# Value matmuls of a head pair in four column groups, with the halves of the sum added on the way back

## The chip, the cores and the metric

The kernel runs on one core of one Trainium2 chip. The metric is the device time of one execution in microseconds. Nothing outside the core takes part: the other cores are idle, and there is no communication.

## The reference, cut to what matters

The program computes a block of four stages on x of shape (4, 512, 128), each with a layernorm before it and a residual add behind it: attention, a routed feed-forward layer of eight experts, a scan, and the feed-forward layer again. The change is in the attention:

```python
q, k, v = (x @ W.T, split into 16 heads of 8) for the three weights
q, k = rope(q), rope(k)
scores = einsum('bhqd,bhkd->bhqk', q, k) / 8 + causal mask
attn = softmax(scores, axis=-1)
out = einsum('bhqk,bhkd->bhqd', attn, v)     # 512 keys, 8 columns per head
x = x + out.transpose @ Wo.T + bo
```

The other three stages come after it and are computed by the same instructions in both kernels.

## The kernel before, in words

**Stages.** Attention takes the first third of the span. It goes through 32 head pairs (`PAIRS`, numbered n = 8a + p for batch a and pair p). Then come the feed-forward layer, the scan and the second feed-forward layer.

**One head pair.** The order is written out by hand in each engine's program. TensorE (PE) does, in the loop over n:

1. `scores(n + 1, 0)` and `scores(n + 1, 1)`: the scores of the next pair, queries on the partitions, only to find each row's maximum on VectorE (DVE, `row_max`, then `split_max`, which writes the maxima into `q_tok`).
2. `queries_with_max(n)`: four transposes of the queries with their maxima (L929 in this place, "Q2T" below). They wait for `split_done`. ScalarE (ACT) copies the result (L703).
3. `weigh_values(n - 1)`: the value matmuls of the pair before (L1003, "V" below). They wait for the last exponentials of that pair.
4. `scores_T(n, 0)`, `scores(n + 1, 2)`, `scores_T(n, 1)`: the transposed scores with the maxima subtracted (L978 with the mask matmuls L983; the first unit is "T0" below, the last "T2"). ACT takes their exponentials (L710) into `probs`.
5. for even n from 2 on, `weighed_T(n // 2 - 1)` (L1012): the transposes of the weighted values of two pairs ("W" below), after ACT has copied them out of PSUM (L715). DVE divides them by the sums (L1405, L1406).
6. `scores_T(n, 2)`, and in some pairs the projections, transposes and output matmuls of the next or the last batch.

**What V computes.** For each of the four key tiles j (512, 384, 256 and 128 query columns, since the mask is causal) and both heads h of the pair, one fp32 matmul with the values as the stationary operand (128 keys x 16 columns: 8 values, a column of ones that gives the softmax sum, zeros) and the probabilities as the moving one. An fp32 matmul is two passes on PE, each a weight load (LDWEIGHTS) and a MATMUL; in the built program both passes of head 0 stand before both passes of head 1. Head h of an even pair writes PSUM partitions 32h to 32h + 15, that of an odd pair 64 + 32h on: one column group of the array for each, so that in a pair two of the four groups are in use. Two pairs (a quad) share the bank `PV_BANK`.

**Slots.** Scores, transposed scores and all other attention results on PE go through a ring of three slots of two PSUM banks each (`RING`), in the order of `ring_order`; PE waits for `slot_free` before it writes and for nothing else there.

**Beside it.** For n < 8 DVE also looks for the maxima of the expert weights (`find_tops`), at n = 10 it sets their scales, and for n = 12 to 27 ACT and DVE split these weights into two parts (L746, L1441). At the end of a batch DVE takes the next layernorm. GpSimd (POOL) does the rotary step of the next batch, and at the start clears the padded tensors, `v_tok` among them (L523, L525). SP issues the loads in one queue, and at their end two fills of `rows_dram` with zeros from a row of `grids` (L472), which are needed by the first scatter after the attention.

Of the kernel before, what the change touches and what calls it, by code (L numbers as in the profile page):

```python
# [25 lines left out]
F = 512  # L26
# [8 lines left out]
HP = H // 2  # L35
# [59 lines left out]
NT = 2 * B * L // P + E - 1  # L95
# [16 lines left out]
SPARE_AT = TOK_AT + B * TT  # L112
FILL_AT = SPARE_AT + NT
GRIDS = FILL_AT + ROW

# [62 lines left out]
def hybrid_block_kernel(nc, x_in, wqkv_in, wo_in, bo_in, w1_in, b1_in, w2_in, b2_in, wg_in, gate_rows_in,  # L178
                        a_in, bm_in, cm_in, dv_in, wdt_in, conv_in, win_in, win_rows_in, wout_in, b1e_in, grids_in,
                        counts_in,  # L180
                        cos_in, sin_in, ident_dram, neg_eye_in, mask_qk_in, mask_kq_in, out):
    with ExitStack() as ctx:  # L182
        def sb(name, shape, dt=F32):
            return ctx.enter_context(nc.sbuf_tensor(name, shape, dt))

        def sem(name):
            return ctx.enter_context(nc.semaphore(name))
# [58 lines left out]
        max_rest = sb("max_rest", [P, TT, 2])  # L246
        v_tok = sb("v_tok", [P, 2, TT, H, VW])

# [27 lines left out]
        tiles_to = sb("tiles_to", [P, E])  # L276
        expert_of = sb("expert_of", [P, NT])
        tiles_past = sb("tiles_past", [P, NT])
        first_row = sb("first_row", [P, NT])
# [3 lines left out]
        list_end = sb("list_end", [P, NT])  # L283
        result_row = sb("result_row", [P, YT])
# [18 lines left out]
        def part(t, at, shape, dt=F32):  # L303
# [4 lines left out]
            return (flat if dt == F32 else flat.bitcast(dt)).rearrange(f"p ({names}) -> p {names}", **sizes)  # L308

        probs_words = probs[:].rearrange("p a b c -> p (a b c)")  # L310
        xf = part(heads_arena, 0, [2, TT, D])
# [28 lines left out]
        b1e = rope_s[:].rearrange("p t d -> p (t d)")[0:3 * E, 0:F]  # L340
        v_words = v_tok[:].rearrange("p a t h w -> p (a t h w)")
        qk_words = qk_sb[:].rearrange("p t d -> p (t d)")
# [44 lines left out]
        goes_to_ready = sem("goes_to_ready")  # L387
        scale_rows_ready = sem("scale_rows_ready")
        zeroed = sem("zeroed")
        post_step = sem("post_step")  # L390
# [30 lines left out]

        attn_loads = [(wqkv, wqkv_in), (cos, cos_in), (sin, sin_in), (neg_eye, neg_eye_in), (mask_qk, mask_qk_in),
                      (mask_kq, mask_kq_in), (wo, wo_in), (bo, bo_in)]
# [19 lines left out]
        def slot_of(unit):  # L443
            return TURN[unit] % RING
# [12 lines left out]
        def _(sp):  # L457
# [9 lines left out]
            for dst, src in scan_loads:  # L467
                sp.dma_start(whole(dst), src).then_inc(scan_in, 16)
            sp.wait_ge(ffn_in, 16 * len(ffn_loads))
            fill = grids[:, FILL_AT:FILL_AT + ROW].bitcast(I32)  # L470
            for r in range(FFNS):
                sp.dma_start(rows_dram[r].ap().rearrange("(n p k) d -> p n (k d)", p=P, k=2),  # L472
                             fill.unsqueeze(1).broadcast_to([P, ROWS // (2 * P), ROW])).then_inc(zeroed, 16)
            sp.wait_ge(slot_free[slot_of(("wo", B - 1))], filled(("wo", B - 1)))
# [34 lines left out]
        def _(pool):  # L509
# [4 lines left out]
            nc.gpsimd.memset(minus_half[:], -0.5).then_inc(pads_set, 1)  # L514
            nc.gpsimd.memset(bias_rows[:].bitcast(I32), 0)
            nc.gpsimd.memset(ones[:], 1.0)
# [179 lines left out]
        def _(act):  # L696
# [198 lines left out]
        def _(pe):  # L895
# [92 lines left out]
            def weigh_values(n):  # L988
                a, p = divmod(n, HP)
                if p == 0:  # L990
                    read_by(("v", a))
                if n == 0:
                    pe.wait_ge(pv_cleared, 1)
                if n >= 2 and n % 2 == 0:
                    pe.wait_ge(weighed_ready, n // 2)
                read_by(("T", n, 2))
                for u in range(3):
                    at = PROB_AT[u]
                    for j in PROB_UNITS[u]:
                        size = L - P * j  # L1000
                        for h in range(2):
                            quadrant = OW * (2 * (p % 2) + h)
                            mm = pe.matmul(ps[quadrant:quadrant + VW, PV_BANK, j * P:L], v_tok[:, a % 2, j, 2 * p + h, :],  # L1003
                                           probs[:, n % 2, h, at:at + size], start=(j == 0), stop=(j == TT - 1))
                        at += size
                mm.then_inc(pv_made, 1)

            def weighed_T(g):
                to = give(("w", g))
                pe.wait_ge(weighed_ready, g + 1)  # L1010
                for t in range(TT):
                    mm = pe.transpose(ps[:, to, t * P:(t + 1) * P], weighed[:, t * P:(t + 1) * P], ident[:])  # L1012
                mm.then_inc(slot_full[slot_of(("w", g))], 1)
# [277 lines left out]
        def _(dve):  # L1291
# [107 lines left out]
            def divide(g):  # L1399
                a, q = divmod(g, 4)  # L1400
                of = take(("w", g))
                if q == 0 and a >= 1:
                    dve.wait_ge(slot_full[slot_of(("at", a - 1))], filled(("at", a - 1)))
                sums = ps[:, of, :].rearrange("p (t h w) -> p t h w", t=TT, h=Q)
# [379 lines left out]
def shape_constants():  # L1784
# [6 lines left out]
    def table(a):  # L1791
        a = np.broadcast_to(a.reshape(TT, P, 1, HD), (TT, P, 2, HD)) * scale
        return a.transpose(1, 0, 2, 3).astype(np.float32)

    def halves(a):
# [15 lines left out]
        "grids": grids, "counts": np.stack([later, np.ones((P, P))], 1).astype(mybir.dt.np(BF16)),  # L1811
        "cos": table(cos), "sin": table(sin), "ident": np.eye(P, dtype=np.float32),
        "neg_eye": halves(NEG_ROOT * np.eye(P)),
# [46 lines left out]
```

## Time and profile before

| | us |
|---|---|
| runs shown | 892.85, 895.38, 888.28 (median 892.85) |
| profiled execution, its own time | 894.25 |
| its span | 892.4 |
| outside the span | 1.85 |
| attention | the first 284 us of the span |
| mean granted TensorE clock | 0.81 of full speed |

The busy shares of the page are averages over four unlike stages. For this change only the attention stage counts, so the views below are of windows inside it. A row of a timeline merges neighbouring instructions of one kind: its first number is the start of the first, the second the time until the modelled end of the last, so the distance between two starts is the safer measure.

### The profile page before, as it was taken

To read this page: it belongs to the slowest core of one execution; us is meant where nothing else is said; L and a number is where in the kernel's file an instruction comes from. 1 tells how busy PE (TensorE), PEld (TensorE's weight loads), DVE (VectorE), ACT (ScalarE), POOL (GpSimd) and SP (SyncE) were. 2 spreads that over 40 slices of the span, in tenths; PEclk is the share of its full clock that TensorE was granted. 3 is DMA by queue.
4 is the path that set the end of the run, shared out by engine and by line. 5 is a ranking of instruction groups with operands and counts; after the bars stand their busy time and mean duration, and the time that the engine had idled before them with its cause. 6 is when DMAs were issued, how large, how long until landed. Compare 5 with 4: busy or idle time off the path is not lost. (4 is left out here: it accounts for less than half of the span.)

```text
span 892.4 us, 16950 instructions
## 1 busy us (share of the span) xinstructions
PE 594.1 (67%) x5836; PEld 402.2 (45%) x5836; DVE 466.1 (52%) x1241; ACT 344.4 (39%) x462; POOL 349.9 (39%) x447
## 2 busy tenths in 40 slices
PE   2588888888885635578776750567676588676730
PEld 1454445444443413466655640234354376555520
DVE  5877776776772555533222221678867543222214
ACT  1355456556652424335332320225254354332310
POOL 4152080190001575534544453114335445444550
PEclk9699999999997757789877785667687799877875
DMA  8995000000000000111110102100000111111104
GB/s 297 328 334 161 2 1 1 1 2 1 1 2 27 24 7 28 38 45 38 31 31 25 37 19 77 35 0 25 7 19 24 35 46 32 31 30 31 35 18 150
DMA packets 45146, 46.37 MB, mean 52 GB/s; under 512 B 5369, under 2 KB 42386, under 8 KB 44810
## 3 DMA queue, kind: packets, MB, share of 16 engines
q1 hardware_dynamic: 40522, 35.91, 13.5%
q0 software_dynamic: 4544, 9.38, 3.1%
q8 instruction: 52, 0.85, 0.4%
q14 instruction: 28, 0.23, 0.1%
HBM read 16.75 MB, written 28.52 MB: 51 GB/s over the span
## 5 line engine op out<-in xcount | busy, mean ns | idle before, releaser
L1650 DVE COPY arena<-ps 128x128 f32<-128x128 f32 x78 | 22.7, 292 | 211.3 <-DMA y_dram<-arena,goes_to 177.4
L831 ACT ACTIVATE arena<-ps,up_back 128x512 f32<-128x512 f32 x78 | 53.6, 687 | 194.5 <-PE ps L1194 194.5
L1194 PE MATMUL ps<-arena,w 128*128 128x128 f16 x936 | 96.6, 246 | 45.3 <-DVE arena L1636 45.0
L1384 DVE TENSOR_REDUCE row_maxima<-ps 128x2 f32<-128x256 f32 (+3 forms) x128 | 99.0, 817 | 42.8 <-PE ps L958 42.5
L710 ACT ACTIVATE probs<-ps 128x768 f32<-128x768 f32 (+1 forms) x96 | 82.5, 884 | 81.2 <-PE ps L983 81.2
L512 POOL TENSOR_TENSOR rstd<-var_eps,minus_half 128x4 f32<-128x4 f32 x16 | 17.0, 1060 | 222.6 <-DVE var_eps L1321 222.6
L1205 PE MATMUL ps<-w,probs 128*128 x936 | 95.2, 248 | 10.8 <-DVE probs L1642 10.7
L1194 PEld LDWEIGHTS ps<-arena,w 128*128 x936 | 72.2, 106 | 65.9 <-issue 55.5
L661 POOL DMA_INDIRECT y_dram<-arena,goes_to x78 | 85.0, 1090 | 34.5 <-POOL goes_to L654 20.9
L643 POOL DMA_INDIRECT rows_dram<-probs,idx x64 | 69.0, 1078 | 52.8 <-DVE idx L1582 33.0
L1205 PEld LDWEIGHTS ps<-w,probs 128*128 128x128 f16 x936 | 77.0, 111 | 21.9 <-issue 12.3
L652 POOL TENSOR_SCALAR result_row<-qk_sb,list_end 128x1 f32<-128x1 f32 x78 | 29.4, 377 | 132.0 <-DMA y_dram<-arena,goes_to 120.9
L1003 PE MATMUL ps<-probs,v_tok 128*16 128x256 f32 (+3 forms) x512 | 74.7, 434 | 2.5 <-ACT probs L710 2.5
L1642 DVE SCALAR_TENSOR_TENSOR probs<-arena,hid_scale,probs 128x512 f16<-128x512 f32 x78 | 58.2, 746 | 4.5 <-ACT probs L836 4.5
L836 ACT ACTIVATE probs<-arena,hid_scale 128x512 f16<-128x512 f32 x78 | 56.3, 721 | 2.6
L1189 PE MATMUL ps<-which,bias_rows 128*128 128x128 bf16 x312 | 37.4, 254 | 20.4 <-issue 20.0
L654 POOL TENSOR_SCALAR goes_to<-result_row,grids 128x1 int32<-128x1 f32 x78 | 46.7, 599 | 7.3
L1003 PEld LDWEIGHTS ps<-probs,v_tok 128*16 128x16 f32 x512 | 24.2, 96 | 47.7 <-issue 35.4
L953 PE MATMUL ps<-heads_arena 48*128 48x128 bf16 (+3 forms) x256 | 37.6, 308 | 11.6 <-DVE row_maxima L1384 6.4
L978 PE MATMUL ps<-q2T,heads_arena 50*128 50x512 bf16 (+3 forms) x256 | 38.5, 310 | 9.0 <-ACT probs L710 7.2
L1189 PEld LDWEIGHTS ps<-which,bias_rows 128*128 128x128 bf16 x312 | 22.1, 112 | 32.2 <-issue 31.4
L1159 PE MATMUL ps<-w,arena 128*128 128x128 f16 x384 | 26.2, 230 | 13.3 <-DVE arena L1616 8.9
(234 smaller groups left out, 1111.7 us busy)
## 6 DMA issues: line engine op xcount, KB each, us to landing
rows_dram<-grids SPq DMA_DIRECT2D x2, 8840.0 KB, 44.1
qk_sb<-rows_dram SPq DMA_DIRECT2D x78, 65.0 KB, 1.8
arena<-in_w SPq DMA_DIRECT2D x2, 2304.0 KB
arena<-y_dram SPq DMA_DIRECT2D x8, 512.0 KB, 4.0
y_dram<-arena,goes_to POOLq DMA_INDIRECT x78, 2.4
x_all<-in_x SPq DMA_DIRECT2D x4, 256.0 KB, 8.1
rows_dram<-probs,idx POOLq DMA_INDIRECT x64
out_x<-x_all SPq DMA_DIRECT2D x4, 256.0 KB, 3.7
```

Of the source, the lines that this page charges most:

```text
L643: nc.gpsimd.indirect_dma_start(rows_dram[r].ap(), bass.IndirectOffsetOnAxis(ap=idx[:, r, b, t, k:k + 1], axis=0), xrow_words[:, b % 2, t, ...
L654: nc.gpsimd.tensor_scalar(goes_to[:, n % YT:n % YT + 1], result_row[:, n % YT:n % YT + 1], grids[:, SPARE_AT + s:SPARE_AT + s + 1], None, ...
L661: nc.gpsimd.indirect_dma_start(y_dram.ap(), bass.IndirectOffsetOnAxis(ap=goes_to[:, n % YT:n % YT + 1], axis=0), y_t[:, n % YT, :], None). ...
L710: nc.scalar.activation(probs[:, n % 2, :, PROB_AT[u]:PROB_AT[u] + size], ps[:, of:of + 2, 0:size], ACT.Exp).then_inc(slot_free[slot_of(("T ...
L831: nc.scalar.activation(hid_t[:, n % HT, :], ps[:, of, :], ACT.Gelu, scale=up_back[:]).then_inc(bank_free[of], 1)
L836: nc.scalar.activation(hid16_t[:, n % HT, 0, :], hid_t[:, n % HT, :], ACT.Identity, scale=hid_scale[:]).then_inc(high_t_ready, 1)
L1003: mm = pe.matmul(ps[quadrant:quadrant + VW, PV_BANK, j * P:L], v_tok[:, a % 2, j, 2 * p + h, :], probs[:, n % 2, h, at:at + size], start=( ...
L1189: pe.matmul(ps[:, to, c * P:(c + 1) * P], bias_rows[:, c * P:(c + 1) * P], which[:, s:s + 1].broadcast_to([P, P]), start=(c == 0), stop=Fa ...
L1194: mm = pe.matmul(ps[:, to, c * P:(c + 1) * P], w1[:, w, bass.ds(expert[s], 1), c * P:(c + 1) * P].rearrange("p o f -> p (o f)"), xgT[:, (r ...
L1205: mm = pe.matmul(ps[:, to, 0:D], hid16_t[:, n % HT, v, c * P:(c + 1) * P], w2[:, w, bass.ds(expert[s], 1), c, :].rearrange("p o d -> p (o ...
L1384: ins = nc.vector.tensor_reduce(row_maxima[:, t, 2 * p:2 * p + 2], ps[:, of:of + 2, o:o + keys], AX.X, ALU.max)
L1642: nc.vector.scalar_tensor_tensor(hid16_t[:, n % HT, 1, :], hid_t[:, n % HT, :], hid_scale[:], hid16_t[:, n % HT, 0, :], ALU.mult, ALU.subt ...
```

## The change

- The values are laid out with 41 words for each key tile and head of two neighbouring pairs: values and a one at 0 to 8 for the even pair, at 32 to 40 for the odd pair, zeros between. The stationary operand is now 32 columns wide. For an even pair it starts at 0, for an odd pair at 16, so that the odd pair's values stand in columns 16 to 24 and zeros in 0 to 15.
- The column group of a matmul is given by head and half of the key tiles: tiles 0 and 3 in one half, 1 and 2 in the other. Both pairs of a quad accumulate into the same four groups.
- Each head's sum then stands in two halves. The way back is no longer a transpose but a matmul with the constant `fold` of ones and zeros (128 x 64), which adds the halves while it turns them. It is an ordinary fp32 matmul, two passes for each of the four query tiles, and writes 64 columns for each tile, not 128.
- ACT copies the values of a batch in two instructions, not one. POOL clears 2640 words of `v_tok`, not 2048, and sets the ones in two instructions.
- `fold` is one more load among the first constants. The zeros for `rows_dram` now come from `bias_rows`, cleared at the start, so that the fills no longer wait for the loads of the feed-forward layer; `grids` is 260 words a row shorter. Four small tables of the tile map share the memory of `weighed`, which is free by then.

```diff
+VS = 2 * VW + HD + 1
+
+HALVES = ((0, 3), (1, 2))
...
-        v_tok = sb("v_tok", [P, 2, TT, H, VW])
+
+        v_flat = sb("v_tok", [P, 2 * TT * HP * VS + VW])
+        v_tok = v_flat[:, 0:2 * TT * HP * VS].rearrange("p (a t g w) -> p a t g w", a=2, t=TT, g=HP)
+        fold = sb("fold", [P, Q * VW])
...
-            sp.wait_ge(ffn_in, 16 * len(ffn_loads))
-            fill = grids[:, FILL_AT:FILL_AT + ROW].bitcast(I32)
+            sp.wait_ge(zero_set, 1)
+            words = ROWS * ROW // (2 * P)
+            size = max(n for n in range(1, F // 2 + 1) if words % n == 0)
+            fill = bias_rows[:, 0:2 * size].bitcast(I32)
...
-            nc.gpsimd.memset(v_tok[:], 0.0).then_inc(pads_set, 1)
+            nc.gpsimd.memset(v_flat[:], 0.0).then_inc(pads_set, 1)
             pool.wait_ge(pads_set, 4)
-            nc.gpsimd.memset(v_tok[:, :, :, :, HD:HD + 1], 1.0).then_inc(pads_set, 1)
+            nc.gpsimd.memset(v_tok[:, :, :, :, HD:HD + 1], 1.0)
+            nc.gpsimd.memset(v_tok[:, :, :, :, 2 * VW + HD:2 * VW + HD + 1], 1.0).then_inc(pads_set, 1)
...
-                nc.scalar.copy(v_tok[:, a % 2, :, :, 0:HD],
-                               ps[:, of, :].rearrange("p (t h d) -> p t h d", t=TT, h=H)).then_inc(slot_free[slot_of(("v", a))], 1)
+                for q in range(2):
+                    ins = nc.scalar.copy(v_tok[:, a % 2, :, :, 2 * VW * q:2 * VW * q + HD].rearrange("p t (g h) d -> p (t g) h d", h=2),
+                                         ps[:, of, :].rearrange("p (g q h d) -> p q g h d", q=2, h=2, d=HD)[:, q])
+                ins.then_inc(slot_free[slot_of(("v", a))], 1)
...
-                for u in range(3):
-                    at = PROB_AT[u]
-                    for j in PROB_UNITS[u]:
-                        size = L - P * j
-                        for h in range(2):
-                            quadrant = OW * (2 * (p % 2) + h)
-                            mm = pe.matmul(ps[quadrant:quadrant + VW, PV_BANK, j * P:L], v_tok[:, a % 2, j, 2 * p + h, :],
-                                           probs[:, n % 2, h, at:at + size], start=(j == 0), stop=(j == TT - 1))
-                        at += size
+                at = {j: PROB_AT[u] + sum(L - P * i for i in PROB_UNITS[u] if i < j) for u in range(3) for j in PROB_UNITS[u]}
+                for j in range(TT):
+                    half = 0 if j in HALVES[0] else 1
+                    for h in range(2):
+                        group = OW * (2 * half + h)
+                        at_v = (((a % 2) * TT + j) * HP + p // 2 * 2 + h) * VS + VW * (p % 2)
+                        mm = pe.matmul(ps[group:group + OW, PV_BANK, j * P:L],
+                                       v_flat[:, at_v:at_v + OW],
+                                       probs[:, n % 2, h, at[j]:at[j] + L - P * j],
+                                       start=(p % 2 == 0 and j == HALVES[half][0]), stop=(j == HALVES[half][1]), skip_group_check=True)
                 mm.then_inc(pv_made, 1)
...
-                    mm = pe.transpose(ps[:, to, t * P:(t + 1) * P], weighed[:, t * P:(t + 1) * P], ident[:])
+                    mm = pe.matmul(ps[:, to, t * Q * VW:(t + 1) * Q * VW], weighed[:, t * P:(t + 1) * P], fold[:], start=True, stop=True)
```

The order of the instructions on PE stays. This is V of a pair in the program before, with what stands around it (the sizes are those of the result, partitions x columns; in brackets the semaphores waited for):

```order
L929 MATMUL ps<-ident,q_tok 128x128 [waits split_done]
L929 MATMUL ps<-ident,q_tok 128x128 x3
L1003 MATMUL ps<-probs,v_tok 16x512 [waits slot_free1]
L1003 MATMUL ps<-probs,v_tok 16x512
L1003 MATMUL ps<-probs,v_tok 16x384 x2
L1003 MATMUL ps<-probs,v_tok 16x256 x2
L1003 MATMUL ps<-probs,v_tok 16x128 x2
L978 MATMUL ps<-q2T,heads_arena 128x512 [waits q2T_ready,slot_free0]
```

And the same place in the changed program, where V is L1012:

```order
L938 MATMUL ps<-ident,q_tok 128x128 [waits split_done]
L938 MATMUL ps<-ident,q_tok 128x128 x3
L1012 MATMUL ps<-probs,v_tok 32x512 [waits slot_free1]
L1012 MATMUL ps<-probs,v_tok 32x512
L1012 MATMUL ps<-probs,v_tok 32x384 x2
L1012 MATMUL ps<-probs,v_tok 32x256 x2
L1012 MATMUL ps<-probs,v_tok 32x128 x2
L987 MATMUL ps<-q2T,heads_arena 128x512 [waits q2T_ready,slot_free0]
```

The tiles come in the same order, two heads each; what differs is that the pairs of 384 and 256 columns now go to the two column groups that the pairs of 512 and 128 leave free.

## Rows read from the trace of the kernel before

**Rows 1.** The page: the span, and the granted TensorE clock in 40 slices.

```profile
span 892.4 us, 16950 instructions
...
PEclk9699999999997757789877785667687799877875
```

**Rows 2.** Stretches: length, busy time by engine (instructions), clock, DMA.

```profile
172.50:281.00 108.50, 90.33 (x1130) 50.65 (x1126) 68.81 (x130) 63.25 (x85) 20.10 (x27) 1.00 0.01 1
281.00:893.00 612.00, 379.27 (x3220) 275.90 (x3220) 271.27 (x842) 201.47 (x279) 272.90 (x340) 0.74 0.12 34
```

**Rows 3.** Timeline of PE, pairs 28 and 29: start, length, instructions [idle before].

```profile
253.64 0.39 PE L978 MATMUL ps<-q2T,heads_arena 50*128 50x512 bf16 x2
...
255.83 0.63 PE L1012 MATMUL ps<-ident,weighed 128*128 128x128 f32 x4 [1.08 <-ACT weighed L715]
256.39 0.28 PE L978 MATMUL ps<-q2T,heads_arena 50*128 50x256 bf16 x2
...
257.96 2.33 PE L1003 MATMUL ps<-probs,v_tok 128*16 128x512 f32 x16
260.22 0.39 PE L978 MATMUL ps<-q2T,heads_arena 50*128 50x512 bf16 x2
...
263.16 0.40 PE L929 MATMUL ps<-ident,q_tok 128*128 128x128 bf16 x4
263.49 2.33 PE L1003 MATMUL ps<-probs,v_tok 128*16 128x512 f32 x16
```

**Rows 4.** Timeline of PE's weight loads inside one V.

```profile
202.47 0.12 PEld L1003 LDWEIGHTS ps<-probs,v_tok 128*16 128x16 f32 x4
202.91 0.10 PEld L1003 LDWEIGHTS ps<-probs,v_tok 128*16 128x16 f32 x2 [0.33 <-issue]
203.34 0.10 PEld L1003 LDWEIGHTS ps<-probs,v_tok 128*16 128x16 f32 x2 [0.33 <-issue]
203.66 0.10 PEld L1003 LDWEIGHTS ps<-probs,v_tok 128*16 128x16 f32 x2 [0.22 <-issue]
```

**Rows 5.** The same V's instructions in a stretch of its first 0.04 us.

```profile
202.46:202.50 0.04, 0.03 (x2) 0.03 (x4) 1.00 0.00 0
```

**Rows 6.** Timeline of PE: eight fp32 passes with 8 and with 128 moving columns.

```profile
302.72 1.06 PE L1120 MATMUL ps<-wg,heads_arena 128*128 128x8 f32 x8
303.64 0.38 PE L1148 MATMUL ps<-ident,route 128*9 128x128 f32 x2
...
243.64 1.16 PE L1026 MATMUL ps<-wo,attT 128*128 128x128 f32 x8
244.73 0.23 PE L953 MATMUL ps<-heads_arena 48*128 48x128 bf16 x2
```

**Rows 7.** Timelines of DVE and ACT beside rows 3.

```profile
261.10 1.22 DVE L1384 TENSOR_REDUCE row_maxima<-ps 128x2 f32<-128x1024 f32 x1 [1.82 <-PE ps L958]
...
262.88 0.18 DVE L1397 CAST q_tok<-max_rest 128x8 bf16<-128x8 f32 x1
...
260.77 2.50 ACT L710 ACTIVATE probs<-ps 128x1024 f32<-128x1024 f32 x3 [2.18 <-PE ps L983]
263.60 0.59 ACT L703 COPY q2T<-ps 128x512 bf16<-128x512 bf16 x1 [0.33 <-PE ps L929]
```

**Rows 8.** Timeline of PE: pairs in which DVE ends the wait behind V.

```profile
102.39 0.39 PE L953 MATMUL ps<-heads_arena 48*128 48x512 bf16 x2 [2.02 <-DVE row_maxima L1384]
...
128.26 0.39 PE L953 MATMUL ps<-heads_arena 48*128 48x512 bf16 x2 [1.17 <-DVE row_maxima L1384]
...
194.82 0.40 PE L929 MATMUL ps<-ident,q_tok 128*128 128x128 bf16 x4 [0.71 <-DVE q_tok L1397]
```

**Rows 9.** Timelines of POOL and PE at the start.

```profile
12.03 1.90 POOL L523 MEMSET v_tok<- 128x2048 f32 x1
...
14.07 0.48 PE L908 MATMUL ps<-ident,xn 128*128 128x128 f32 x1 [1.18 <-DVE xn L1327]
```

**Rows 10.** The instructions of ACT's copy of the values: duration min/median/max.

```profile
L728 ACT COPY v_tok<-ps x4: 586/591/592, 19.7 to 180.1; 128x512 f32<-128x512 f32 x4
```

More of the change, by code:

```diff
@@ L112 @@
 SPARE_AT = TOK_AT + B * TT
-FILL_AT = SPARE_AT + NT
-GRIDS = FILL_AT + ROW
+GRIDS = SPARE_AT + NT
 BANKS = 8
@@ L180, in hybrid_block_kernel @@
                         counts_in,
-                        cos_in, sin_in, ident_dram, neg_eye_in, mask_qk_in, mask_kq_in, out):
+                        cos_in, sin_in, fold_in, ident_dram, neg_eye_in, mask_qk_in, mask_kq_in, out):
     with ExitStack() as ctx:
@@ L308, in part @@
             return (flat if dt == F32 else flat.bitcast(dt)).rearrange(f"p ({names}) -> p {names}", **sizes)
+        expert_of, tiles_past, first_row, list_end = (weighed[:, NT * i:NT * (i + 1)] for i in range(4))
         probs_words = probs[:].rearrange("p a b c -> p (a b c)")
@@ L340, in hybrid_block_kernel @@
         b1e = rope_s[:].rearrange("p t d -> p (t d)")[0:3 * E, 0:F]
-        v_words = v_tok[:].rearrange("p a t h w -> p (a t h w)")
+        v_words = v_flat[:]
         qk_words = qk_sb[:].rearrange("p t d -> p (t d)")
@@ L388, in hybrid_block_kernel @@
         scale_rows_ready = sem("scale_rows_ready")
+        zero_set = sem("zero_set")
         zeroed = sem("zeroed")
@@ L420, in hybrid_block_kernel @@
         out_dram = out.rearrange("b (t p) d -> b p t d", p=P)
-        attn_loads = [(wqkv, wqkv_in), (cos, cos_in), (sin, sin_in), (neg_eye, neg_eye_in), (mask_qk, mask_qk_in),
+        attn_loads = [(wqkv, wqkv_in), (cos, cos_in), (sin, sin_in), (fold, fold_in), (neg_eye, neg_eye_in), (mask_qk, mask_qk_in),
                       (mask_kq, mask_kq_in), (wo, wo_in), (bo, bo_in)]
@@ L468, in _ @@
                 sp.dma_start(whole(dst), src).then_inc(scan_in, 16)
-            sp.wait_ge(ffn_in, 16 * len(ffn_loads))
-            fill = grids[:, FILL_AT:FILL_AT + ROW].bitcast(I32)
+            sp.wait_ge(zero_set, 1)
+            words = ROWS * ROW // (2 * P)
+            size = max(n for n in range(1, F // 2 + 1) if words % n == 0)
+            fill = bias_rows[:, 0:2 * size].bitcast(I32)
             for r in range(FFNS):
-                sp.dma_start(rows_dram[r].ap().rearrange("(n p k) d -> p n (k d)", p=P, k=2),
-                             fill.unsqueeze(1).broadcast_to([P, ROWS // (2 * P), ROW])).then_inc(zeroed, 16)
+                sp.dma_start(rows_dram[r].ap().rearrange("(p k) d -> p (k d)", p=P).rearrange("p (n w) -> p n w", w=size),
+                             fill.unsqueeze(1).broadcast_to([P, words // size, size])).then_inc(zeroed, 16)
             sp.wait_ge(slot_free[slot_of(("wo", B - 1))], filled(("wo", B - 1)))
@@ L514, in _ @@
             nc.gpsimd.memset(minus_half[:], -0.5).then_inc(pads_set, 1)
-            nc.gpsimd.memset(bias_rows[:].bitcast(I32), 0)
+            nc.gpsimd.memset(bias_rows[:].bitcast(I32), 0).then_inc(zero_set, 1)
             nc.gpsimd.memset(ones[:], 1.0)
@@ L1403, in divide @@
                     dve.wait_ge(slot_full[slot_of(("at", a - 1))], filled(("at", a - 1)))
-                sums = ps[:, of, :].rearrange("p (t h w) -> p t h w", t=TT, h=Q)
+                sums = ps[:, of, 0:TT * Q * VW].rearrange("p (t h w) -> p t h w", t=TT, h=Q)
                 core_link(nc.vector.reciprocal(rec[:], sums[:, :, :, HD]))
@@ L1811, in shape_constants @@
         "grids": grids, "counts": np.stack([later, np.ones((P, P))], 1).astype(mybir.dt.np(BF16)),
-        "cos": table(cos), "sin": table(sin), "ident": np.eye(P, dtype=np.float32),
+        "cos": table(cos), "sin": table(sin),
+        "fold": np.tile(np.eye(Q * VW, dtype=np.float32).reshape(2, 2, VW, Q * VW).transpose(1, 0, 2, 3).reshape(Q * VW, Q * VW), (2, 1)),
+        "ident": np.eye(P, dtype=np.float32),
         "neg_eye": halves(NEG_ROOT * np.eye(P)),
```

4 lines of the change are left out of this document (removed).

## The prediction

> **What bounds the kernel now.** I began with the page: the span, the clock and the shares [rows 1]. The shares mix four stages, so the next view was busy time by stretch. In 108.5 us of attention PE is busy for 90.3, DVE for 68.8, ACT for 63.3, at full clock; behind 281 the clock is granted at 0.74 on average [rows 2]. Nothing in that second part is changed, so it should only move forward. The question is whether attention ends earlier.
>
> The timeline of PE answers what a pair costs [rows 3]. From the T0 of pair 28 to that of pair 29 it is 260.22 - 253.64 = 6.58 us (even pairs, with W), and from V to V one pair on 263.49 - 257.96 = 5.53 (odd pairs). V holds PE from 257.96 to the next T0 at 260.22, thus 2.26 us of each, and T0 stands right behind it. The views of DVE and ACT beside it [rows 7] show the loop: T0 at 260.22, exponentials from 260.77 to 263.27, maxima split at 262.88 + 0.18 = 263.06, Q2T at 263.16, V at 263.49. All of this hangs on T0; V alone hangs on nothing but its place, and T0 on V. So a shorter V shortens the loop one for one, until something that does not hang on T0 is late.
>
> **V itself.** Its weight loads show the steps [rows 4]: four at 202.47, two at 202.91, 203.34 and 203.66, each pair with the start of a pass in both heads. A pass takes 0.43 us for 512 columns (both steps) and 0.32 for 384; so 0.215 and 0.11 for 256 and 128 by the same rate. Before, a group has all eight passes: 2 x (0.43 + 0.32 + 0.215 + 0.11) = 2.15, and 0.11 until T0 starts. After, heads' groups of tiles 0 and 3 have 2 x (0.43 + 0.11) = 1.08, those of tiles 1 and 2 have 2 x (0.32 + 0.215) = 1.07. If all four groups run at once V takes **1.08 + 0.11 = 1.2 us, 1.07 less**. The trace never has more than two groups at work, so bounds: 1.2 from below (each group must do its passes); 2.26 from above, since no more is asked than that heads keep running side by side as now. The weight loads are 32 columns for 16; they lie under the passes.
>
> Whether the groups run at once depends on order. In the program both passes of head 0 come before head 1, yet two passes start within the first 0.04 us and four weight loads with them [rows 5]: head 1's first pass went past head 0's second, which waited for its own group. With four groups it has to go past two and three waiting passes. The Trainium skill, "TensorE: Matmul & The Clock Gate", Part 3, The mechanism, says instead that matmuls are "pc-monotone in start AND end", in strict order. By that rule the steps would be a chain in which only neighbours overlap, and V would stay near what it is. The start of two passes of different heads in 0.04 us speaks against it, so I take 1.2. A middle case is that only two passes may wait in front: then tiles 1 and 2 start at 0.43, and V ends after 0.43 + 2 x 0.32 + 2 x 0.215 + 0.11 = 1.6 us.
>
> V is on the path in 32 pairs: 32 x 1.07 = **34.2 us** at most.
>
> **W.** The transposes hold PE from 255.83 to 256.39, 0.56 us for four single passes [rows 3]. The new ones are eight fp32 passes with a 128-column stationary operand and 64 moving columns. Eight with 8 moving columns take 303.64 - 302.72 = 0.92, eight with 128 take 244.73 - 243.64 = 1.09 [rows 6]: the weight load, not the moving side, sets the step of about 0.11. I take 1.0 (the bounds are these two rows), 0.44 more. W stands on the path: T2 waits behind it, the last exponential behind T2, V behind that. 16 x 0.44 = **7.0 us back** (5.8 to 8.5). The same page's table of terms calls transpose mode "4× faster for FP32". By that, W would take 4 x 0.56 = 2.24 and the price be 27 us; rows 6 have an ordinary fp32 tile at twice a transpose, not four times, because the load bounds both.
>
> In the quad's other chain, DVE divides 0.44 later. In pair 28 its results are due when the third slot of the scores is given out, about the time it gets there now; I put up to 0.05 on it, nothing in the sum.
>
> **Where the 1.07 does not arrive.** With V shorter, work that does not shrink comes to the front.
> - At two batch ends DVE is the path behind V: S waits 2.02 us for it at 102.39, from a chain of layernorm and weight maxima begun before V [rows 8]; a like wait stands at the second end. At 128.26 it waits 1.17 for the scales set at n = 10. V's gain there is lost whole: 3 x 1.07 = 3.2.
> - Elsewhere DVE sits idle before its last maximum. Where that is over 1.07 (1.82 at 261.10 [rows 7]) nothing is lost, and ACT has room too: its query copy ends at 263.60 + 0.59 = 264.19, V now would end at 264.7. In pairs with weight splits or maxima on DVE the idle time is shorter; the worst case is at 194.82, where Q2T already waits 0.71 for DVE [rows 8]. Going pair by pair I lose about 0.8 there, 0.5 before the first batch end, 0.3 and 0.1 in two others, and 1 us for backlogs in n = 3 to 7 and 19: 2.8 in all.
>
> Sum of losses: **6 us** (4 to 9).
>
> **The small edits.** The larger `v_tok` costs at the start: the clearing takes 1.90 us for 2048 words, and only behind it does DVE give the last piece of the first layernorm to PE at 14.07 [rows 9]. 2640 words take 2.45: **+0.55**, on the path (nothing else is ready). The two settings of ones lie behind that piece. ACT's copy of the values, 0.59 us four times [rows 10], becomes two of half the size, each with its fixed part: between +0 and +0.59 each, I take 0.2 for three batches in pairs that are not bound by ACT, so **+0.3**. `fold` is one more small load in a queue whose constants are in before PE gets to them. The zero fills start where their queue gets to them instead of behind the loads, which are nearly done by then; they are needed hundreds of us later. Nothing for either.
>
> **Sum.** -34.2 + 7.0 + 6 + 0.8 = -20.4. The profiled execution has 894.25, so 873.9 for it; it lies 1.4 above the median of the runs shown, so against the median **873 us** (0.978).
>
> **Rivals.**
> - *Two passes may wait, not three* (V 1.6, 0.66 less): 32 x 0.66 = 21.1, of which DVE takes 2.6, so -21.1 + 2.6 + 7.0 + 0.8 = -10.7: 882. For it: the trace shows one pass passed, no more. 14%.
> - *No overlap beyond now, slower*: V stays at 2.26 and the new groups only change places. Then W and the start are left, +7.0 + 0.8: **901**. It decides from a V above 2.0 (32 x 0.24 = 7.8). For it is the page's rule of strict order; against it rows 5. 8%.
> - *Transposes cheap by four*: W at 2.24, 16 x 1.68 = 27 in place of 7: 893. Against it rows 6. 3%.
> - *The clock*: with less to do PE might fall to the lower of its two levels inside attention, as it does at the batch ends, where it had waited 2.02 for DVE [rows 1, 8]. A pair has about 4 us of PE work then, at half clock 8, so eight such pairs cost 8 x 3.5 = 28, all of the gain: about 901. Against it: even pairs with 1.08 us of waiting keep full clock now. 4%.
> - *DVE takes more*, 12 us instead of 6, because its chains slip together: 879. 8%.
>
> My forecast, four groups at once with these losses, has the remaining 63%, its own range 868 to 878 (W 5.8 to 8.5, losses 4 to 9, runs that spread by 7 us). To hold 8 in 10, the range reaches over the DVE case and most of the middle one: **868 to 884**. What a measurement here can tell from no change is about 1%, thus 883.9 and 901.8. Faster by more: all of the forecast and the DVE case, two thirds of the middle one: 0.79. Within 1%: the rest of the middle one, half of the slower ones, the transposes: 0.13. Slower: 0.08.
>
> **What the profile after would show.** V to T0 in 1.2 us (middle case 1.6), four first passes and up to eight weight loads in its first 0.05 us. W as x8 in 1.0. Odd pairs at 4.5 in place of 5.53, even ones at 5.95 in place of 6.58. The same waits at the ends of the batches, a little longer, since PE comes earlier. Attention ends near 264, not 284, and what follows takes as long as now. I am wrong if V keeps its length, if the clock falls inside a batch, or if waits for DVE or ACT stand before most T1 or V.

## The result and the profile after

The changed kernel takes **883.7 us** (median of 19 runs, 877.3 to 890.6), the kernel before, measured beside it, 891.7: ratio **0.990 [0.988, 0.993]** (the brackets hold a 95% interval). It is faster, but by 8 us and not by the 20 of the forecast. The profiled execution has 887.59 against 894.25, spans 885.8 and 892.4.

The page first, as in [rows 1]:

```profile
span 885.8 us, 17084 instructions
...
PEclk9699899888996767699777775758677799777765
```

A slice is 22 us. In slices 3 to 12, which are attention, stand four 8s where [rows 1] has ten 9s: the granted clock falls inside attention. To keep the start apart from it I read attention from the V of pair 0, V(0), to that of pair 31, V(31). Busy time by stretch, columns as in [rows 2], of before and then of the change:

```profile
45.91:275.37 229.46, 191.93 (x2409) 110.18 (x2407) 160.99 (x320) 131.96 (x172) 63.85 (x86) 0.99 0.16 48
```

```profile
47.53:268.25 220.72, 181.16 (x2468) 120.75 (x2467) 162.37 (x320) 132.44 (x175) 63.92 (x86) 0.91 0.34 61
```

Attention is 8.7 us shorter, at a granted clock of 0.91, not 0.99. V(0) comes 1.6 us later, and from V(31) to the end of the span it is 617.0 us before and 0.5 more now. So -8.7 + 1.6 + 0.5 = -6.6, the span's difference. Nearly all that is missing is missing inside attention.

Is it V? PE's timeline of pairs 28 and 29, as in [rows 3]:

```profile
256.63 1.28 PE L1012 MATMUL ps<-probs,v_tok 128*32 128x512 f32 x16
257.85 0.39 PE L987 MATMUL ps<-q2T,heads_arena 50*128 50x512 bf16 x2
...
260.04 1.08 PE L1022 MATMUL ps<-fold,weighed 128*128 128x64 f32 x8 [1.08 <-ACT weighed L722]
261.05 0.28 PE L987 MATMUL ps<-q2T,heads_arena 50*128 50x256 bf16 x2
```

V to T0 is 257.85 - 256.63 = 1.22 (2.26 in [rows 3]), and W to T2 1.01 (0.56). The weight loads of another V, to be read against [rows 4]:

```profile
97.13 0.16 PEld L1012 LDWEIGHTS ps<-probs,v_tok 128*32 128x32 f32 x8
97.49 0.64 PEld L1012 LDWEIGHTS ps<-probs,v_tok 128*32 128x32 f32 x8 [0.21 <-issue]
```

Eight loads at once where there were four. And V's instructions alone, in its first 0.05 us, against [rows 5]:

```profile
97.12:97.17 0.05, 0.04 (x4) 0.04 (x6) 1.00 0.54 106
```

Four passes where there were two: all four groups are at work. So V and W are as forecast.

Now the place where the clock falls, PE's timeline at the first end of a batch, against [rows 8]:

```profile
98.57 0.28 PE L992 MATMUL ps<-mask_kq,neg_eye 64*128 64x128 bf16 x4
101.93 0.39 PE L962 MATMUL ps<-heads_arena 48*128 48x512 bf16 x2 [3.08 <-DVE row_maxima L1394]
...
103.44 1.97 PE L1022 MATMUL ps<-fold,weighed 128*128 128x64 f32 x8
105.33 0.40 PE L987 MATMUL ps<-q2T,heads_arena 50*128 50x256 bf16 x2
```

PE gets to the wait 1 us sooner, so it waits 3.08 us where it waited 2.02; a little later, at half the clock, the same eight instructions of W take 1.89 us, not 1.01. Four stretches in the view by windows: the wait, what follows it, and two later ones.

```profile
98.35:101.93 3.58, 0.50 (x11) 0.21 (x8) 3.55 (x11) 1.50 (x2) 1.02 (x1) 1.00 1.15 206
105.33:109.00 3.67, 3.67 (x39) 2.63 (x38) 1.34 (x4) 1.40 (x2) 0.38 (x1) 0.50 1.15 195
163.70:167.10 3.40, 3.03 (x20) 2.13 (x20) 2.91 (x6) 0.81 (x1) 0.68 (x1) 0.50 0.02 5
191.00:204.70 13.70, 12.51 (x106) 7.30 (x102) 8.80 (x17) 5.86 (x9) 7.26 (x10) 0.50 0.01 2
```

PE is busy for 0.50 us of the 3.58 in which it waits, and after the fall all the time at 0.50, which is the lower of its two levels, 1.2 GHz. Six such stretches add up to 37.5 us in attention; before there were two, 6.8 us. The longest, 191.0 to 204.7, follows no long wait but short ones (0.97 us until 188.47, 0.36 until 189.33, 0.28 until 190.47).

### The profile page after: what moved, and what is told of

Same layout as the page of the kernel before. It is cut to its first block and busy times, and to the rows that moved or that the text cites. A ratio compares the mean times of both kernels' runs of the same rounds, so it can differ in the third digit from the quotient of the medians.

```text
span 885.8 us, 17084 instructions
## 1 busy us (share of the span) xinstructions
PE 585.2 (66%) x5900; PEld 415.3 (47%) x5900; DVE 467.5 (53%) x1241; ACT 345.0 (39%) x466; POOL 349.8 (39%) x448
## 5 line engine op out<-in xcount | busy, mean ns | idle before, releaser
L1394 DVE TENSOR_REDUCE row_maxima<-ps 128x2 f32<-128x256 f32 (+3 forms) x128 | 98.5, 817 | 26.2 <-PE ps L967 25.6
L1215 PE MATMUL ps<-w,probs 128*128 x936 | 96.0, 250 | 10.8 <-DVE probs L1652 10.4
L518 POOL TENSOR_TENSOR rstd<-var_eps,minus_half 128x4 f32<-128x4 f32 x16 | 17.0, 1061 | 209.8 <-DVE var_eps L1331 209.8
L668 POOL DMA_INDIRECT y_dram<-arena,goes_to x78 | 83.7, 1073 | 32.6 <-POOL goes_to L661 20.9
L659 POOL TENSOR_SCALAR result_row<-qk_sb,weighed 128x1 f32<-128x1 f32 x78 | 30.3, 388 | 141.6 <-DMA y_dram<-arena,goes_to 129.0
L962 PE MATMUL ps<-heads_arena 48*128 48x128 bf16 (+3 forms) x256 | 39.8, 324 | 17.3 <-DVE row_maxima L1394 11.6
L1012 PE MATMUL ps<-probs,v_tok 128*32 128x256 f32 (+3 forms) x512 | 45.4, 476 | 2.3 <-ACT probs L717 2.3
L987 PE MATMUL ps<-q2T,heads_arena 50*128 50x512 bf16 (+3 forms) x256 | 40.7, 326 | 8.4 <-ACT probs L717 4.5
L967 PE MATMUL ps<-mask_qk,neg_eye 64*128 64x128 bf16 x512 | 36.8, 229 | 0.0
L992 PE MATMUL ps<-mask_kq,neg_eye 64*128 64x128 bf16 x512 | 34.8, 230 | 0.0
```

The source lines that it names most:

```text
L659: link(nc.gpsimd.tensor_scalar(result_row[:, n % YT:n % YT + 1], xg_words[:, n % XG, D:D + 1], list_end[:, s:s + 1], xg_words[:, n % XG, D ...
L668: nc.gpsimd.indirect_dma_start(y_dram.ap(), bass.IndirectOffsetOnAxis(ap=goes_to[:, n % YT:n % YT + 1], axis=0), y_t[:, n % YT, :], None). ...
L1215: mm = pe.matmul(ps[:, to, 0:D], hid16_t[:, n % HT, v, c * P:(c + 1) * P], w2[:, w, bass.ds(expert[s], 1), c, :].rearrange("p o d -> p (o ...
L1394: ins = nc.vector.tensor_reduce(row_maxima[:, t, 2 * p:2 * p + 2], ps[:, of:of + 2, o:o + keys], AX.X, ALU.max)
```

## Why does DVE keep PE waiting?

DVE's timeline in pair 2 (L1394 the row maxima, L1404 to L1407 their split for the queries), and under it POOL's in the same stretch, where it rotates the next batch's q and k:

```profile
61.40 3.01 DVE L1394 TENSOR_REDUCE row_maxima<-ps 128x2 f32<-128x256 f32 x4
64.54 1.01 DVE L1404 CAST q_tok<-row_maxima 128x8 bf16<-128x8 f32 x1
65.58 1.06 DVE L1405 TENSOR_TENSOR max_rest<-row_maxima,q_tok 128x8 f32<-128x8 f32 x1
66.68 0.19 DVE L1407 CAST q_tok<-max_rest 128x8 bf16<-128x8 f32 x1
```

```profile
64.35 1.16 POOL L584 TENSOR_TENSOR rope_s<-rope_c,q_tok 128x512 f32<-128x512 f32 x1
65.46 1.15 POOL L585 TENSOR_TENSOR rope_s<-rope_c,k_tok 128x512 f32<-128x512 f32 x1
66.68 0.65 POOL L586 CAST q_tok<-rope_s 128x512 bf16<-128x512 f32 x1
```

Two instructions on eight columns take 1.01 and 1.06 us, and each ends when POOL's does: 64.54 + 1.01 = 65.55 beside 64.35 + 1.16 = 65.51, then 66.64 beside 66.61. The third begins together with POOL's next, at 66.68, and takes 0.19. The four row maxima take 3.01 us beside POOL, and as much where POOL is idle (experiment 7). That is what the Trainium skill, "SBUF — State Buffer", Who interferes with whom, says: the port pair that DVE shares with GpSimd goes to whoever issues first, for the whole instruction, and the other side is fully blocked; among DVE's instructions casts can ask for it, those with two operands in SBUF meet GpSimd's reads there, and reductions don't contend. The trace agrees. Before, the same split took 0.28, 0.62 and 0.54, behind a longer V. Whether this matters is a question for runs.

So the theory is: V and W are right; shorter pairs bring PE to waits that DVE sets, the waits grow, and the clock's falls take about half of what is missing. The rival is that V's gain is worth less than its length (PE shares something when four groups run), or that the fold or the fills cost more than their instructions.

## The experiments

Each ratio is to the kernel before as it was measured beside that kernel: 894.5 us for experiments 1 to 3 and the changed kernel of 4, 893.3 for the control of 4, the first two kernels of 7 and experiment 8, 900.8 for the others. "Attention" is V(0) to V(31) of the profiled execution, and a "half-rate stretch" is one in it at a granted clock of 0.50. Every edit but the control's and the first of 7 is made to the changed kernel.

**1. Two groups, with the fold.** The group goes by head alone.

```diff
-                    half = 0 if j in HALVES[0] else 1
+                    half = 0
...
-                                       start=(p % 2 == 0 and j == HALVES[half][0]), stop=(j == HALVES[half][1]), skip_group_check=True)
+                                       start=(p % 2 == 0 and j == 0), stop=(j == TT - 1), skip_group_check=True)
```

> The changed kernel with one part undone: the column group of a value matmul is given by the head alone, so V has two groups again; fold, layout, start and fills stay as changed. If W and the start were sized right (7.0 and 0.8 us), this is 8 us above the kernel before (ratio 1.009), V takes 2.26 us up to T0 again and W 1.0; the clock then stays full inside a batch as before. If W costs less than thought because its 0.44 us lie beside the waits for DVE, the ratio is 1.003 or below. If the clock falls here too (theory of the clock wrong: it does not come from the shorter V), PE shows half rate in more than the two stretches at the batch ends.

907.3 us, **1.017 [1.013, 1.021]**; even pairs take 7.04, not 6.58 (+0.46). Without four groups the fold is a loss, and larger than expected: 15 x 0.45 = 6.8 us are its length, and the clock costs more here too (attention 237.92 at 0.97 on average, 233.25 with the clock held in experiment 5, so 4.7). The value of four groups is the distance to the change, 1.017 - 0.990.

The expectation had the clock as before. It falls at the same two places, the ends of the batches, and behind the same wait (2.01 us at the first, 2.02 before), but each stretch is twice as long, 13.7 us in all and not 6.8. This is the first:

```profile
104.00:110.70 6.70, 6.34 (x54) 4.70 (x52) 3.45 (x9) 2.21 (x3) 0.38 (x1) 0.50 1.15 198
```

So a part of what the clock costs comes with the other edits (the fold, the start, the copies) and not with the shorter V.

**2. Four groups, no fold.** W is a transpose again.

```diff
-                    mm = pe.matmul(ps[:, to, t * Q * VW:(t + 1) * Q * VW], weighed[:, t * P:(t + 1) * P], fold[:], start=True, stop=True)
+                    mm = pe.transpose(ps[:, to, t * P:(t + 1) * P], weighed[:, t * P:(t + 1) * P], ident[:])
...
-                sums = ps[:, of, 0:TT * Q * VW].rearrange("p (t h w) -> p t h w", t=TT, h=Q)
+                sums = ps[:, of, :].rearrange("p (t h w) -> p t h w", t=TT, h=2 * Q)[:, :, 0:Q, :]
```

> The changed kernel with the four transposes in place of the fold matmuls: the adding of the two halves is left out, half of the sums is divided. W goes back from 1.0 to 0.56 us. Plain pairs: even ones at 5.5 us in place of 5.98. If W is on the path everywhere, 7 us less than the changed kernel (ratio 0.982). If the longer waits of PE for DVE now lower the clock more often, less of it arrives: ratio 0.985 to 0.990, with more time at half rate inside attention than the 38 us of the changed kernel.

877.1 us, **0.983 [0.980, 0.985]**. Even pairs 5.53 in place of 5.98: 0.45 x 16 = 7.2, and 0.0077 x 892 = 6.9 by the ratios, give or take 3. Attention falls by more, from 220.7 to 209.9, since less of it is at half rate: 17 us in four stretches, not 37.5 in six. So what shows W's term is the length of W and of the plain pairs, and the total is only in line with it. The clock falls in more places than before without the fold as well, so the fold is not what starts that; but it lengthens it.

**3. The old shape of the fills.** The zeros come from a wide cleared tile again, at the early place in the queue.

```diff
-            fill = bias_rows[:, 0:2 * size].bitcast(I32)
+            fill = zero_rows[:].bitcast(I32)
...
+                sp.dma_start(rows_dram[r].ap().rearrange("(n p k) d -> p n (k d)", p=P, k=2),
+                             fill.unsqueeze(1).broadcast_to([P, ROWS // (2 * P), ROW])).then_inc(zeroed, 16)
```

> The changed kernel with the zero fills in their old shape (1040 bytes a piece instead of 884, in rows interleaved over the partitions, from a zero row widened by 16 bytes), started where the changed kernel starts them. The fills then end near 86 us again, not near 110. If the longer fills disturb nothing, the ratio is that of the changed kernel, 0.990 within 0.003. If they slow the start or the weights' way, 1 to 3 us less, and V of the first pair starts near 46 us in place of 47.5.

886.2 us, **0.991 [0.989, 0.994]**: the same as the change. Attention took 220.73 in its profile and 220.72 in the change's. The new shape costs nothing, and the two numbers also say how exactly attention repeated here. The earlier place was not undone; in the traces the fills start at 21.4 in the change and at 22.0 before.

**4. The clock held.** Idle matmuls (results never read), 109 in all, where PE waits for DVE by about as long anyway: in loops 4, 5, 8, 11, 16, 19, 20. A control does it to the kernel before, in loops 4, 8, 11, 16.

```diff
+            def keep_busy(n, count):
+                for _ in range(count):
+                    pe.matmul(ps[:, Q2_BANK, (n + 1) % 2 * (L // 2):((n + 1) % 2 + 1) * (L // 2)], ident16[:],
+                              kT[:, n // HP % 2, 0, 0:L // 2], start=True, stop=True)
...
                 scores_T(n, 0)
+                keep_busy(n, {8: 26, 16: 26, 11: 22, 19: 6}.get(n, 0))
...
+                    keep_busy(n, {5: 12}.get(n, 0))
                     scores(n + 1, 1)
+                keep_busy(n, {4: 12, 20: 5}.get(n, 0))
```

> The changed kernel with idle matmuls of 256 bf16 columns (0.107 us each, results overwritten) put where PE waited longest for DVE: 26 in pairs 8 and 16, 22 in pair 11, 6 in pair 19 before the scores of the next pair, 12 and 5 before the query transposes of pairs 4 and 20, 12 in pair 5. Theory of the clock: the changed kernel loses about 10 us to 38 us at half rate inside attention (before 7 us), because PE waits longer; kept busy, the clock stays full, attention ends 8 to 10 us earlier, ratio 0.979 to 0.982. Rival, DVE and GpSimd: the time is lost because DVE is the path in those pairs whatever PE's clock; then the ratio stays at 0.990 or gets worse by what the idle matmuls delay, even with the clock at 1.0.

> Control: the kernel before with idle matmuls in its own longest waits for DVE (17 in pairs 8 and 16, 10 in pair 11, 6 before the query transposes of pair 4). It loses only 7 us to half rate inside attention, so the theory of the clock gives it 1 to 3 us (ratio 0.996 to 1.000), far less than the 11 us that idle matmuls gave the changed kernel. If it gains as much as that one (0.987), the gain there is no matter of what the change did to the clock.

The changed kernel: 874.7 us, **0.978 [0.974, 0.981]**. The control: 889.7 us, 0.996 [0.993, 0.999]. More work for PE makes the changed kernel 1.3% faster. PE's timeline at the same end of a batch, the idle matmuls in place of the wait of 3.08:

```profile
96.03 0.39 PE L987 MATMUL ps<-q2T,heads_arena 50*128 50x512 bf16 x2
96.26 0.28 PE L992 MATMUL ps<-mask_kq,neg_eye 64*128 64x128 bf16 x4
96.47 3.01 PE L1041 MATMUL ps<-heads_arena,ident 128*128 128x256 bf16 x26
99.62 0.39 PE L962 MATMUL ps<-heads_arena 48*128 48x512 bf16 x2
```

and its attention as a stretch:

```profile
46.69:257.37 210.68, 180.11 (x2578) 122.42 (x2576) 164.48 (x320) 132.20 (x175) 63.88 (x86) 0.99 0.37 64
```

From T0 to the next S it is 3.59 us here and 3.58 in the change: DVE sets that time, PE idle or not. But pair 7 as a whole falls from 12.01 to 9.27, pair 15 from 11.88 to 9.43, and attention from 220.7 to 210.7: **10.0 us** of the change are half rate. Before, the control's attention is 228.8 against 229.5, 0.7.

Neither hold is complete. Here one stretch is left, 251.3 to 254.7, and the last step, V(30) to V(31), takes 5.57 us, where it takes 4.25 at full clock in experiments 2 and 9: 1.3 more. In the control the two ends of a batch gain 2.4 (10.26 to 9.11 and 10.47 to 9.26), but a stretch that was not there before begins at 131.8, and one V in it takes 3.74 us and not 2.27. Put right by these, the clock costs the change 11.3 us and the kernel before 2.2: still 9 between them.

**5. Two groups with the clock held** prices V by itself: experiment 1 with 50 idle matmuls.

```diff
-                    half = 0 if j in HALVES[0] else 1
+                    half = 0
...
+                keep_busy(n, {4: 6}.get(n, 0))
...
+                keep_busy(n, {8: 17, 16: 17, 11: 10}.get(n, 0))
```

> Column groups by head only (two at once, as before the change) with the fold kept, and idle matmuls at PE's long waits, so that the clock is held: against 'warm' only the value matmuls differ in the clock-free comparison. If four groups save the 1.07 us of each V to T0 step on the plain path, it is 27 to 33 us above 'warm', ratio 1.008 to 1.015. If with the clock held the gain of four groups were as small as the 8.7 us of the change as a whole plus the fold's 7, it would be 16 us above 'warm', ratio 0.996.

909.6 us, 1.011 [1.006, 1.016]. Its clock stays up through all of attention:

```profile
47.06:280.31 233.25, 201.69 (x2519) 125.09 (x2517) 160.02 (x320) 131.74 (x175) 63.90 (x86) 1.00 0.33 58
```

and V is as long as ever (84.07 to the T0 at 86.35, 2.28):

```profile
84.07 2.35 PE L1012 MATMUL ps<-probs,v_tok 128*32 128x512 f32 x16
86.35 0.39 PE L987 MATMUL ps<-q2T,heads_arena 50*128 50x512 bf16 x2
```

233.3 - 210.7 = 22.6 us, or 23.9 without the stretch that experiment 4 has left, is what four groups give at full clock. The 31 steps are worth 31 x (2.28 - 1.22) = 32.9, so 9 to 10 stand in waits that do not shrink. By ratio it is (1.011 - 0.978) x 892 = 30 us, give or take 5, as expected, but against two measurements of the kernel before, 900.8 and 894.5; why it lies above the traces I can't say, and I take the traces, in which plain pairs agree to 0.02 us. Against the control, 228.8 less 1.5 for its stretch, the fold costs 6.0 us at full clock, near its 6.8. Either way four groups gain more than they seem to in the change as a whole, and the rival of a V that is worth less falls.

**6. Halves with unequal columns.** It asks what sets V's length: tiles 0 and 1 in one half, 2 and 3 in the other.

```diff
-HALVES = ((0, 3), (1, 2))
+HALVES = ((0, 1), (2, 3))
```

> Key tiles 0 and 1 in one half, 2 and 3 in the other, in place of 0 and 3, 1 and 2: the columns of one half are then 512+384 against 256+128 instead of 640 each. If the four groups run side by side and the longest sets the time, V takes 896/640 of what it does: T0 starts 1.6 us after V instead of 1.22, over 31 pairs 9 to 12 us, 893 to 896 us in all, ratio 1.000 to 1.004. If V's time goes by the sum of the columns (the engine takes them one behind another), nothing changes: ratio 0.990.

898.4 us, 0.998 [0.995, 1.000], just under the 1.000 to 1.004 expected. V to T0 is 85.67 - 84.04 = 1.63:

```profile
84.04 1.70 PE L1012 MATMUL ps<-probs,v_tok 128*32 128x512 f32 x16
85.67 0.39 PE L987 MATMUL ps<-q2T,heads_arena 50*128 50x512 bf16 x2
```

The longest group sets V, by its own passes: 2 x (0.43 + 0.32) + 0.11 = 1.61 from the prices of [rows 4]. Plain pairs took 0.41 more, thus up to 12.7 us; by the ratios it is 6.7 us in all, and in attention 4.2, at a clock of 0.95, not 0.91 (21 us at half rate, not 37.5). The length of a step and what it moves in the clock work against each other here.

```profile
48.38:273.29 224.91, 186.03 (x2468) 115.50 (x2467) 162.19 (x320) 132.20 (x175) 63.91 (x86) 0.95 0.33 59
```

**7. Without the rotation on POOL.** The rotary step of batches 1 to 3 is left out, which leaves POOL idle beside DVE.

```diff
-                for t in range(TT):
-                    qk = qk_sb[:, t, :].rearrange("p (k h d) -> p k h d", k=2, h=H)
...
-                nc.gpsimd.tensor_tensor(k_slot(4), kr, k_slot(1), ALU.subtract).then_inc(roped, 1)
+                nc.gpsimd.memset(k_tok[:, 0, 0, 0:1], 0.0).then_inc(roped, 1)
```

> The kernel before without the rotary step of batches 1 to 3 on GpSimd (left out; these batches work on old queries and keys). Theory: small DVE instructions wait while GpSimd works, but in the kernel before most of that is hidden behind V: 1 to 4 us less, ratio 0.995 to 0.999.

> The changed kernel without the rotary step of batches 1 to 3 on GpSimd (left out). Theory of DVE and GpSimd: pairs 3, 4, 11 and 19, where DVE is the path, lose 5 us to DVE instructions that wait for GpSimd, and the drops of the clock behind them another 5; without it the ratio to the kernel before is 0.978 to 0.982 (10 us below the changed kernel), against 1 to 4 us for the same edit in the kernel before. If only the clock at the batch ends matters, 1 to 3 us as there.

> The changed kernel without the rotation of batches 1 to 3 on GpSimd (their q and k are those of batch 0), and idle matmuls only in loops 8 and 16, where PE waits for VectorE by 3 us. It leaves VectorE alone on its port where the rotation stood beside it. Without either, the changed kernel lost 15 us with the rotation taken out and 9 us with the clock held. If the rotation costs mostly by making PE wait until the gate falls, the two overlap: 868 to 871 us, ratio 0.974 to 0.977. If VectorE's slow small instructions cost by themselves, they add up: 860 to 865 us, ratio 0.965 to 0.970.

Before: 887.2 us, 0.993 [0.991, 0.996]. The change: 871.2 us, 0.974 [0.969, 0.978]. The change with idle matmuls in loops 8 and 16: 865.3 us, **0.960 [0.956, 0.965]**. So by the ratios the rotation costs the kernel before 6 us and the changed one 15 (0.9902 - 0.9737); in the traces attention itself loses 3.7 before (229.5 to 225.7). All three ratios lie below the figures that were expected, and the last says that clock and rotation are in the main separate losses: 0.0126 and 0.0165 one by one, 0.0299 together. With the clock held the rotation makes attention 210.7 - 199.9 = 10.8 us longer. The split of pair 2 without it, and attention:

```profile
63.53 0.19 DVE L1376 CAST q_tok<-row_maxima 128x8 bf16<-128x8 f32 x1
63.75 0.17 DVE L1377 TENSOR_TENSOR max_rest<-row_maxima,q_tok 128x8 f32<-128x8 f32 x1
63.96 0.19 DVE L1379 CAST q_tok<-max_rest 128x8 bf16<-128x8 f32 x1
...
46.75:246.66 199.91, 173.10 (x2521) 117.73 (x2519) 150.81 (x320) 131.74 (x175) 5.75 (x8) 0.99 0.38 68
```

0.17 to 0.19 where it was up to 1.06. Pair 2 takes 4.53, with the rotation 6.32, clock held in both; pairs 3, 10, 18 and 19 are shorter by 1.6, 3.4, 1.9 and 1.1. DVE's busy time in attention falls from 164.5 to 150.8. These kernels leave POOL's rotation out as a whole; a rotation that only leaves the port alone was not tried, so that the port is the cause rests on the ends that coincide above.

**8. The start.** POOL clears q_tok, k_tok and v_tok only when the four normalized tiles are there.

```diff
+            pool.wait_ge(xna_ready, TT)
             nc.gpsimd.memset(q_tok[:].bitcast(I32), 0)
```

> The changed kernel, but GpSimd clears q_tok, k_tok and v_tok only once DVE has made the first layernorm (a wait in front of the three). In the changed kernel these clearings hold DVE's four instructions until 14.5 us, 2.4 of it by the larger v_tok. Expected: xn ready at 8 us, PE starts 6 us earlier; the rotary step on DVE then waits for the clearings, which end 1 to 2 us later than now. Net 2 to 4 us less than the changed kernel, ratio 0.986. If all is hidden behind the first loads, no change.

881.9 us, **0.985 [0.980, 0.991]**, an interval that overlaps the change's, and V(0) at 42.3, not 47.5. (The 2.4 us in the expectation are the whole clearing of `v_tok`; its growth is 0.5.) DVE's timeline, in the change and then in this run:

```profile
6.58 7.90 DVE L1337 TENSOR_SCALAR xn<-x_all,mean,rstd 128x128 f32<-128x128 f32 x4 [0.96 <-POOL rstd L518]
```

```profile
6.70 1.12 DVE L1338 TENSOR_SCALAR xn<-x_all,mean,rstd 128x128 f32<-128x128 f32 x4 [0.96 <-POOL rstd L518]
13.49 0.42 DVE L1354 TENSOR_TENSOR rope_c<-ps,cos 128x256 f32<-128x256 f32 x1 [5.68 <-POOL k_tok L529]
```

Four normalizations take 1.12 us alone and 7.90 beside POOL's clears. V(0) comes 5.3 us earlier and the span is 8.6 us shorter than the change's; by the ratios it is 4.3, give or take 5, so that a gain in time is likely but not shown. Four half-rate stretches, 23.9 us, remain.

**9. All that the runs point to.** Idle matmuls as in 4 (with 8 more in loop 30 and 12 ahead of the last V) and the later clears.

> The version that the runs so far point to: the changed kernel, with the idle matmuls of the run 'warm' (plus 8 ahead of the fold of loop 30 and 12 ahead of the last value matmuls, where PE stood longest before the gate fell late in attention), and GpSimd clearing q_tok, k_tok and v_tok only after the four normalized token tiles are there. If the gate and the start are separate losses, they add up: 'warm' took 9 us off the changed kernel and the later clears alone 1.7 to 4 us (V(0) 5 us earlier, part of it lost to more half-rate clock), so 869 us, ratio to before 0.972 to 0.976, V(0) at 42.3 us. If the earlier start only makes the attention wait at the next transfer or for GpSimd's rotation, the ratio stays at warm's 0.978.

877.2 us against 900.8, **0.973 [0.969, 0.978]**: the fastest version that computes everything, 1.7% under the change as it stands. V(0) is at 42.6, attention 209.8. Against experiment 4 the intervals overlap, so the start's share is not settled by it.

## Why the prediction was wrong

The forecast was 873 and the time is 883.7: 20.4 us were promised, and 8.0 came by the medians, 8.7 by the ratio. The time lies at the very end of the stated range, 868 to 884. That is luck: the range reached so far for a V of 1.6 us and for a DVE that takes 12 us, and neither came. The step that failed is the clock inside attention, which the sum has at nothing; it measures 9 us. Step by step, for the profiled execution:

| step | forecast, us | measured, us | from |
|---|---|---|---|
| V, 31 pairs | -33.2 | -32.6 | 2.27 to 1.22 |
| W, 15 between V(0) and V(31) | +6.6 | +6.8 | 0.56 to 1.01; experiment 2 |
| waits that V's gain runs into | +6 | +7.7 | what is left: 228.8 - 210.7 = 18.1 = 32.6 - 6.8 - 7.7 |
| clock inside attention | 0 | **+9.4** | 10.0 now, 0.7 before |
| start, and ACT's copies | +0.85 | +1.6 | V(0), see below; the copies of batches 1 to 3 are in the row of waits |
| behind V(31) | -0.6 | +0.5 | 617.0 before |

Measured sum -6.6, as the spans have it.

- **V** was right, and for the reason given: all groups at once, the longest sets the length (experiment 6 has the other value, 1.63, within 0.02 of the same prices). The rivals of two waiting passes and of strict order fall: four passes are at work in the first 0.05 us, and the rule of strict order that the prediction cites is not borne out by this trace.
- **W** was right in its length, 1.01 for 1.0. The rival of a transpose four times cheaper falls too: the factor is 1.8.
- **Waits for DVE** come out within their bounds of 4 to 9, as what is left when the other rows are taken off (experiment 5 has 9 to 10). They grow where the prediction put them, but a part of their cause, small instructions that POOL holds up, was not in it. I had read 1.82 us of DVE idle time in pair 29 as room, where POOL does not work.
- **The clock** is the step that failed. I gave it 4%, with the words "even pairs with 1.08 us of waiting keep full clock now". That was the wrong row to ask. The one to ask was [rows 8]: in the kernel before the clock falls behind a wait of 2.02, and the change lengthens just this wait by what it takes off V, to 3.08. My own sentence "the same waits at the ends of the batches, a little longer" holds this cause, and I put no price on it. Nor did I see that the other edits would matter to the clock: with V as long as before, experiment 1 has 13.7 us at half rate in two places and pays 4.7 for it; with the short V and no fold, experiment 2 has 17 in four; both together make 37.5 in six. So the shorter V brings the new places, and more comes with the fold. The price I had for the rival (28 us) was wrong in the other direction: half rate costs little where DVE or ACT sets the pace, 11 us in 37.5. "If the clock falls inside a batch" was one of my signs of being wrong, and it is the one that came.
- **The start**: the last piece reaches PE 0.47 later, as forecast. V(0) is 1.6 later in this profile, but in the others with the same start it is at 46.5 to 48.4, and the two with the old start have 46.7 and 47.7, before itself 45.9. Beyond the 0.5 nothing is shown.
- **Slips in the sums**: -20.4 from 892.85 is 872.5, not 873, and the list of chances gives 0.80, 0.14 and 0.06, not 0.79, 0.13 and 0.08. Neither matters here.
- **Fills**: nothing for their new shape, as forecast, though they run longer (below).

## What to carry to other kernels

A change that shortens the busiest engine's work lengthens its waits where another engine sets their end (2.02 to 3.08 here). So list the longest waits of PE before, add the gain to each, and ask whether the clock, which already fell behind one of them, will fall behind them all. Price the half-rate stretches by what PE alone decides there, not by their length. A step made longer can cost clock as well, so price such a step with the clock held. And idle time of DVE is room only where POOL is not working beside it: read DVE's smallest instructions in that stretch.

## What was not expected of the hardware

- Adding 109 idle matmuls to PE in attention made the kernel 1.3% faster, by the clock.
- DVE's instructions on 8 columns took 1.0 us beside POOL's work and 0.17 to 0.19 without, and four normalizations 7.90 and 1.12.
- The half-rate stretches at the two ends of a batch last 6.8 us each with the fold (the change, experiments 1, 6 and 8) and 3.4 each with transposes (before, experiment 2). But the kernel before without the rotation has 6.8 and 3.4, with transposes too, so the longer W is not needed for it, and what decides the length stays open.
- The zero fills in their new shape held their queue's instructions 39.8 us where it was 23.6, and cost nothing that experiment 3 can show; they are needed far later:

```profile
21.37 39.80 SPq L478 DMA_DIRECT2D rows_dram<-bias_rows  x2
```
